# Feed-forward residual path earlier, softmax sums of the first block inverted once per value, six places for weight sums

## What is computed

```python
x = x + layernorm(attention(layernorm(x)))   # 16 heads of 16, weights alpha * sign(W), bias
x = x + layernorm(ffn(x))

def ffn(x):                                  # ternary weights, one scale per output
    h = silu(lin(x, w1)) * lin(x, w2)        # 256 -> 1024
    h = gelu(lin(h, h1))                     # 1024 -> 1024
    h = gelu(lin(h, h2))                     # 1024 -> 1024
    return lin(h, w3)                        # 1024 -> 256
```

## Time and profile before

| | us |
|---|---|
| median of three runs | 1197.16 |
| profiled execution, own time | 1199.53 |
| its span, first to last instruction | 1197.8 |
| PE busy | 1145.4 (96%) |
| ACT busy | 918.6 (77%) |
| DVE busy | 755.8 (63%) |
| last exponential of attention ends | about 549 |
| a middle feed-forward block | 80.2 |

### The profile page before, as it was taken

One profiled execution on the slowest core, in us unless ns is written; L12 is line 12 of the kernel. 1 busy time (PEld: TensorE's weight loads), 2 busy tenths in 40 slices (PEclk: granted clock), 3 DMA queues, 4 the chain that ended last, 5 costly groups with the idle time before them and its releaser, 6 DMA issues.

```text
span 1197.8 us, 21087 instructions
## 1 busy us (share of the span) xinstructions
PE 1145.4 (96%) x8241; PEld 778.0 (65%) x8241; DVE 755.8 (63%) x1165; ACT 918.6 (77%) x1218; POOL 88.6 (7%) x140
## 2 busy tenths in 40 slices
PE   6699999999999999898999999999999999999997
PEld 4233323332333322225999999989989999899897
DVE  7354525353436246895767767768678677686766
ACT  6689999999999999795675676757756766577565
POOL 6001000101010000000010000010100000101000
PEclk9799999999999999899999999999999999999999
DMA  5989768976899589834330431423404314233031
GB/s 180 238 213 230 190 103 194 225 182 103 198 212 202 103 187 199 221 123 152 100 138 30 142 125 61 151 92 110 141 35 141 125 55 145 101 110 138 4 124 55
DMA packets 67031, 166.96 MB, mean 139 GB/s; under 512 B 10102, under 2 KB 27126, under 8 KB 60774
## 3 DMA queue, kind: packets, MB, share of 16 engines
q1 hardware_dynamic: 66636, 165.12, 51.2%
q10 hardware_dynamic: 288, 0.39, 0.1%
HBM read 122.18 MB, written 52.40 MB: 146 GB/s over the span
## 4 chain that ended last, share of the span: by engine, by line
PE 32%; DVE 10%; ACT 6%; issue 3%; POOL 2%; DVEq 0%; ACTq 0%
PE ffn_ps L1876 21%; DVE op_lo L2130 4%; PE ffn_ps L1814 4%; PE ffn_ps L1815 4%; ACT op_hi L1991 3%; PE ffn_ps L1889 3%; ACT feed L2020 2%; PE side_ps L1781 1%; DVE feed L2123 1%; ACT zn L2026 1%; DVE ln_stats L2108 1%; DVE feed L2148 1%; ACT L2020 1%; POOL ln_shift L1701 1%; DVE feed L2141 1%
## 5 line engine op out<-in xcount | busy, mean ns | idle before, releaser
L1286 ACT ACTIVATE probs<-s_ps 128x1024 f32<-128x1024 f32 x512 | 475.5, 1115 | 36.0 <-PE s_ps L1131 35.4
L1145 PE MATMUL y_ps<-probs,v_st 128*17 128x512 f32 x2048 | 272.7, 605 | 9.1 <-DVE y_sb L1311 8.1
L1876 PE MATMUL ffn_ps<-op_hi,W 128*128 128x256 f32 x1024 | 240.5, 279 | 0.0
L1876 PE MATMUL ffn_ps<-op_lo,W 128*128 128x256 f32 x1024 | 240.5, 279 | 0.0
L2130 DVE TENSOR_TENSOR op_lo<-feed,op_hi 128x1024 fp32r<-128x1024 f32 x144 | 174.7, 1222 | 95.3 <-ACT op_hi L1991 95.3
L1131 PEld LDWEIGHTS s_ps<-q_st,k_st 50*128 50x128 f32 x1024 | 88.4, 187 | 209.9 <-ACT probs L1286 172.0
L1131 PE MATMUL s_ps<-q_st,k_st 50*128 50x512 f32 x1024 | 207.4, 470 | 7.8 <-DVE y_ps L1521 7.3
L1876 PEld LDWEIGHTS ffn_ps<-op_hi,W 128*128 128x128 f32 x1024 | 193.3, 189 | 0.3
L1876 PEld LDWEIGHTS ffn_ps<-op_lo,W 128*128 128x128 f32 x1024 | 191.7, 187 | 0.3
L1876 PE MATMUL ffn_ps<-op_hi,sums_of_w 128*128 128x256 f32 x768 | 186.8, 284 | 0.5 <-ACT feed L2007 0.5
L1876 PE MATMUL ffn_ps<-op_lo,sums_of_w 128*128 128x256 f32 x768 | 186.0, 283 | 0.0
(11 more groups left out here) (199 smaller groups left out, 1308.8 us busy)
## 6 DMA issues: line engine op xcount, KB each, us to landing
sums_of_w<-sum_scr SPq DMA_DIRECT2D x48, 1024.0 KB, 5.0
k_st<-qk_scr SPq DMA_DIRECT2D x90, 128.0 KB, 6.5
q_st<-qk_scr SPq DMA_DIRECT2D x90, 128.0 KB, 7.0
w_scr<-ffn_w SPq DMA_DIRECT2D x16, 704.0 KB, 8.0
W<-w_scr SPq DMA_DIRECT2D x16, 704.0 KB, 5.9
y_scr<-y_sb SPq DMA_DIRECT2D x32, 256.0 KB, 4.0
qk_scr<-y SPq DMA_DIRECT2D x24, 256.0 KB, 6.8
qk_scr<-sums SPq DMA_DIRECT2D x24, 256.0 KB, 7.9
```

The source lines that it names most:

```text
L1145: i = pe.matmul(y_ps[32 * j:32 * j + VCOLS, :], v_st[g % 2][:, s, VCOLS * j:VCOLS * (j + 1)], probs[(PAIRS * turn + j // 2) % PROBS][:, j ...
L1286: act.activation(probs[a % PROBS][:, :, :], s_ps[a % 3][:, :, :], ACT.Exp, scale=SCALE)\
L1876: mm = pe.matmul(dst[:, a * HB:(a + 1) * HB], w, part[slot][:, kt // 2, cols].bitcast(form), start=(fresh and kt == 0 and a == 0 and part ...
```

## The change

It has three parts.

1. `sum_at` has six places for the first 16 sums: the two new ones lie in the tile `zn`. Three semaphores instead of two tell of stored sums; `wait_sum_stores` waits for the first so many pairs of them. At turn 36, before `zn` is written with the projection, DVE waits for the first six pairs.
2. For the first block the sums are loaded once per value, 128 x 64 (`load_few_sums`), DVE inverts them with one instruction at turn 22, and at turn 24 SP waits for that, stores them in `inv_scr`, waits for the store and loads them spread over the rows, as the later blocks do. The four spread inversions and their two loads at turn 11 go.
3. In the feed-forward blocks the steps of the residual path take earlier places: on PE `project_y` from behind U2 to behind Z of layer 0, and `turn_x1` from between the two output pairs to behind C21 of layer 1; on ACT `normalise(Z)` from behind high(13) to behind high(10), `normalise(X1)` from behind high(15) to behind high(13), and the high part of x1 from behind high(17) to between the two gelus of Q12; on DVE the low part of y to behind low(3), and with it low(3) to before both halves of `add_c11`; scaling, bias, statistics, adding x and the low part of x1 as the diff shows. SP's order in these blocks is the same; its code moves into shared functions.

```diff
@@ -154,34 +154,38 @@
+def load_few_sums(sp, y_scr, few_sums, b, u, done):
+
+    y_blk = y_scr.rearrange("(b c a d) t -> b c a d t", b=BATCH, c=CT, d=2 * HEAD_DIM)
+    for c in range(CT):
+        few = y_blk[b, c, :, HEAD_DIM, u * BLK:(u + 1) * BLK].rearrange("a (s f) -> a s f", s=HEAD_DIM // 2)
+        sp.dma_start(few_sums[c * HALF:(c + 1) * HALF, :], few).then_inc(done, 16)
+
+
 def load_tail_y(sp, y_scr, tail_in, b, u):
     y_blk = y_scr.rearrange("(b c a d) t -> b c a d t", b=BATCH, c=CT, d=2 * HEAD_DIM)
-    tokens = slice(u * BLK, (u + 1) * BLK)
     for c in range(CT):
-        sp.dma_start(tail_in.y[:, c, :], y_blk[b, c, :, 0:HEAD_DIM, tokens]).then_inc(tail_in.y_loaded, 16)
-
-        sp.dma_start(tail_in.sums[:, c, :], y_blk[b, c, :, HEAD_DIM:HEAD_DIM + 1, tokens]
-                     .to_broadcast([P // HEAD_DIM, HEAD_DIM, BLK])).then_inc(tail_in.y_loaded, 16)
+        sp.dma_start(tail_in.y[:, c, :], y_blk[b, c, :, 0:HEAD_DIM, u * BLK:(u + 1) * BLK]).then_inc(tail_in.y_loaded, 16)
+
+
+def store_inverses(sp, inv_scr, few_sums, done):
+    sp.dma_start(inv_scr.rearrange("h (s f) -> (h s) f", s=HEAD_DIM // 2), few_sums).then_inc(done, 16)
+
+
+def spread_inverses(sp, inv_scr, tail_in):
+    for c in range(CT):
+        heads = HEADS // CT
+        sp.dma_start(tail_in.sums[:, c, :], inv_scr[c * heads:(c + 1) * heads, :].unsqueeze(1)
+                     .to_broadcast([heads, HEAD_DIM, BLK])).then_inc(tail_in.y_loaded, 16)
 TAIL_LOADS = 2 * CT
-
-
-INVERT_PARTS = 4
-
-
-def invert_sums(dve, tail_in, t, part):
-
-    if part == 0:
-        dve.wait_ge(tail_in.y_loaded, 16 * TAIL_LOADS * (t + 1))
-    n = CT * BLK // INVERT_PARTS
-    sums = tail_in.sums[:, :, :].rearrange("p c t -> p (c t)")[:, part * n:(part + 1) * n]
-    dve.reciprocal(sums, sums).then_inc(tail_in.inverted, 1)
+FEW = HEADS * BLK // P
 def divide_y(dve, tail_in, t):
-    dve.wait_ge(tail_in.inverted, INVERT_PARTS * (t + 1))
+    dve.wait_ge(tail_in.y_loaded, 16 * TAIL_LOADS * (t + 1))
     dve.tensor_tensor(tail_in.y[:, :, :], tail_in.y[:, :, :], tail_in.sums[:, :, :], ALU.mult)\
         .then_inc(tail_in.y_done, 1)
...
@@ -793,6 +797,7 @@
         qk = [sb(f"pj_qk{u}", [P, BLK], F32) for u in range(2)]
         group_top = sb("pj_group_top", [P, GROUPS], F32)
+        few_sums = group_top[:, 0:FEW]
         square = sb("pj_square", [P, QK, GROUPS], BF16)
         v_aug = sb("pj_v_aug", [P, HEADS // QUAD, TILES, QUAD, VCOLS], F32)
@@ -856,7 +861,9 @@
         sum_made = sem("sum_made")
         sum_checked = sem("sum_checked")
-        sum_stored = [sem(f"sum_stored{i}") for i in range(2)]
+        sum_stored = [sem(f"sum_stored{i}") for i in range(3)]
+        few_loaded = sem("at_few_loaded")
+        inv_stored = sem("at_inv_stored")
         Y_HI, Y_LO, Z_SCALED, Z_BIASED, Z_ADDED = 1, 2, 3, 5, 6
         block = ctx.enter_context(nc.Block())
@@ -874,9 +881,19 @@
         def sum_at(j):
-            if j % 4 < 2:
-                return qk[j % 4][:, :]
-            return v_aug[:, :, :, :, :].rearrange("p q t j n -> p (q t j n)")[:, (j % 4 - 2) * HM:(j % 4 - 1) * HM]
+            n = j % 6 if j < SUM_UNITS // 2 else j % 4
+            if n < 2:
+                return qk[n][:, :]
+            if n < 4:
+                return v_aug[:, :, :, :, :].rearrange("p q t j n -> p (q t j n)")[:, (n - 2) * HM:(n - 1) * HM]
+            return xb[:, :, :].rearrange("p t c -> p (t c)")[:, (n - 4) * HM:(n - 3) * HM]
+
+        def wait_sum_stores(eng, pairs):
+
+            for r in range(3):
+                n = len(range(r, pairs, 3))
+                if n:
+                    eng.wait_ge(sum_stored[r], 32 * n)
         def quarter_of_w(l, kt, m, k):
...
@@ -1008,7 +1025,13 @@
                     for i in range(2):
                         sp.wait_ge(part_stored[i], 16 * 2 * (QK // 2) * PROJECTED)
+                    load_few_sums(sp, y_scr, few_sums, 0, 0, few_loaded)
                     load_tail_y(sp, y_scr, tail_in, 0, 0)
+                if t == 24:
+                    sp.wait_ge(tail_in.inverted, 1)
+                    store_inverses(sp, inv_scr, few_sums, inv_stored)
+                    sp.wait_ge(inv_stored, 16)
+                    spread_inverses(sp, inv_scr, tail_in)
                 if t == 26:
                     sp.dma_start(tail_in.x1[:, :, :], x_blk[0]).then_inc(tail_in.x_loaded[0], 16)
...
@@ -1444,8 +1466,7 @@
                 a11, a12, a21, a22 = (quarter_of_w(l, kt, m, k) for m, k in ((0, 0), (0, 1), (1, 0), (1, 1)))
                 dst, prior = sum_at(j), sum_at(j - 1)
-                if j >= 4:
-                    dve.wait_ge(sum_stored[j // 2 % 2], 32 * (j // 4))
+                wait_sum_stores(dve, j // 2 - (2 if j < SUM_UNITS // 2 else 1))
                 if j:
                     dve.wait_ge(sum_made, j)
@@ -1471,8 +1492,9 @@
                 if t in SUM_TURNS:
                     sum_of_weights(SUM_TURNS.index(t))
-                if t in (24, 26, 28, 30):
-                    invert_sums(dve, tail_in, 0, (t - 24) // 2)
+                if t == 22:
+                    dve.wait_ge(few_loaded, 16 * CT)
+                    dve.reciprocal(few_sums, few_sums).then_inc(tail_in.inverted, 1)
                 if t == 32:
                     divide_y(dve, tail_in, 0)
@@ -1482,6 +1504,8 @@
                     dve.tensor_tensor(y_lo[:, :, :], tail_in.y[:, :, :], y_hi[:, :, :].bitcast(F32),
                                       ALU.subtract).then_inc(x1_steps, 1)
+                if t == 36:
+                    wait_sum_stores(dve, 6)
                 if t in (36, 38):
                     i, per_bank = (t - 36) // 2, TILES // CT
...
@@ -1927,13 +1942,14 @@
                 for k in range(NP):
                     product(i, 0, k)
-                    if ahead and k == K_U2:
+                    if ahead and k == K_Z:
                         project_y(i)
                 for k in range(NP):
                     product(i, 1, k)
+                    if ahead and k == K_C21:
+                        turn_x1(i)
                 if ahead:
                     out_tiles(i, 0)
-                    turn_x1(i)
                     out_tiles(i, 1)
                 else:
@@ -2070,6 +2086,8 @@
                 copy_c11(i, 1, 1)
                 high(i, 10)
+                if ahead:
+                    normalise(Z, i + 1, zn, zn, z_norm)
                 gelu(i, 1, Q11, 0)
                 gelu(i, 1, Q11, 1)
@@ -2080,21 +2098,19 @@
                 high(i, 13)
                 if ahead:
-                    normalise(Z, i + 1, zn, zn, z_norm)
+                    normalise(X1, i + 1, zn, x1[1 - u], x1_norm)
                 gelu(i, 1, Q22, 0)
                 gelu(i, 1, Q22, 1)
                 gelu(i, 1, Q21, 1)
                 high(i, 15)
+                gelu(i, 1, Q12, 0)
                 if ahead:
-                    normalise(X1, i + 1, zn, x1[1 - u], x1_norm)
-                gelu(i, 1, Q12, 0)
+                    high_of_x1(i)
                 gelu(i, 1, Q12, 1)
                 high(i, 16)
                 high(i, 17)
-                if ahead:
-                    high_of_x1(i)
             blocks(step)
@@ -2175,10 +2191,6 @@
                 dve.wait_ge(few_loaded, 16 * CT * (i + 1))
                 dve.reciprocal(few_sums[:, :], few_sums[:, :]).then_inc(few_inverted, 1)
-
-            def divide(i):
-                dve.wait_ge(tail_in.y_loaded, 16 * TAIL_LOADS * (i + 2))
-                dve.tensor_tensor(y[:, :, :], y[:, :, :], tail_in.sums[:, :, :], ALU.mult).then_inc(y_done, 1)
             def low_of_y(i):
@@ -2270,15 +2282,17 @@
                 make_t(i, 0, 2)
                 if ahead:
-                    divide(i)
+                    divide_y(dve, tail_in, i + 1)
                 make_t(i, 0, 3)
+                low(i, 3)
+                if ahead:
+                    low_of_y(i)
                 add_c11(i, 0, 0)
-                low(i, 3)
                 add_c11(i, 0, 1)
                 make_t(i, 0, 4)
                 low(i, 4)
                 if ahead:
-                    low_of_y(i)
+                    scale_z(i)
                 low(i, 5)
                 if behind:
@@ -2286,17 +2300,16 @@
                 add_c22(i, 0, 1)
                 if ahead:
-                    scale_z(i)
+                    bias_z(i)
                 low(i, 7)
                 if ahead:
-                    bias_z(i)
                     dve.wait_ge(z_done, i + 1)
                     stats_of(Z, zn, range(TILES))
                 add_c12(i, 0, 0)
                 low(i, 8)
-                add_c12(i, 0, 1)
                 if ahead:
                     mean_var_of(Z, i + 1)
+                add_c12(i, 0, 1)
                 make_t(i, 1, 1)
                 low(i, 9)
@@ -2306,24 +2319,25 @@
                 make_t(i, 1, 4)
                 low(i, 11)
+                if ahead:
+                    add_x(i, 1 - u, ahead[0])
                 low(i, 12)
+                if ahead:
```

(12 more changed lines are left out.)

31 lines of the change are left out of this document (11 added, 20 removed).

## The result

The changed kernel takes 1225.98 us (median of four runs, 1221.75 to 1229.84) against 1196.75 us (1195.18 to 1197.98) for the kernel before on the same chip: 1.0244 times as long, 95% interval 1.0207 to 1.0281. The forecast was 1214.7 with a range to 1224. The sign was right, the size was 11 us short, and the median lies 2 us outside the range. One run further down, of the kernel with one wait filled, took 1375.79 us at a mean granted clock of 0.75 and is in no median.

A forecast was written before the change was run, and what follows sets the result against it. The matrix engine was taken to bound the feed-forward part, ACT's exponentials the attention part. Terms -7.2 + 10.4 + 0.3 + 14.0 = +17.5 us on a median of 1197.2 gave 1214.7 us, range 1200 to 1224.

The forecast's parts named there:

- Attention: Attention part: gaps of 4.68 and 0.66 us close and 1.8 us of the other four goes; gain 7.2 us.
- Layer 0: Feed-forward blocks 1 to 6: add_c11 behind low of y delays U2's copy and U3; loss 1.73 us each, 10.4 us together.
- Layer 1: Feed-forward, seven blocks: second output pair released later, its gap growing from 1.5 to about 2.8 us; loss 2.0 us each, 14.0 together.
- The string: Layer 1: ACT's unbroken work from normalising x1 at 697.28, crossing DVE twice, puts the second output pair at 711.30.
- POOL's part: Layer 1: normalising x1 waits for POOL's rstd and shift, 2.89 us after mean and variance end.
- the rule: POOL contends with two-input SBUF instructions on VectorE: first POOL item would wait for low(13), sum the same within 0.1 us.
- rival D: Widened gap before the second output pair lowers the clock: 1.7 us per block, 1226 us if in each; chance 0.12.
- My gap of 2.8 us: Forecast idle time of PE before layer 1's second output pair, about 2.8 us where it was 1.5.
- the likeliest case: The forecast itself, whole kernel: +17.5 us, 1214.7 us; chance 0.60.
- A: Layer 1 goes as meant, -0.9 us per block, while layer 0 costs 10.7: 1194.4 us; chance 0.13.
- B: Nothing is lost in layer 0 and layer 1 is won: 1183 us; chance 0.07.
- C: Layer 0 is free, layer 1 costs 14 us: 1204 us; chance 0.08.

## Why the prediction failed, point by point

- Attention: -7.2 forecast, -7.3 in the profiled pair, -5.0 by the ratio of medians. That the pair agrees to 0.1 us is in part luck, since another trace with the attention part of before ends it 2.65 us sooner. The gaps of 4.68 and 0.66 us closed, and of the other four 1.5 of 3.5 us went (0.47, 0.93 and 0.67 are left), where I took 1.8. The copy of turn 33 was forecast near 481 and came at 481.22; the division, forecast with the spreads at 477 to 479, started at 478.20. Where I was wrong without consequence: I had both edits work together, and either does it alone.
- Layer 0: 1.73 us per block forecast, 1.76 measured. The copy of U2 started at 660.44, that is 665.97 with 5.53 us added (forecast 665.99), and U3 likewise at 666.70 (forecast 666.72). The projection before them idled 0.10 us and not 0.3. The cause is shown by the kernel with add_c11 first. Block 0 has no such wait, as forecast, and in block 7 it grew from 0.52 to 0.80.
- Layer 1: 2.0 us per block forecast, 1.78 measured (83.74 - 80.20 - 1.76), of which 0.63 + 2.40 - 1.48 = 1.55 stand in the listed waits. ACT started normalising x1 after 3.9 us idle, forecast some 4. With 5.53 us added and layer 0's 1.73 taken off it began at 697.10 (forecast 697.28), and the second pair at 711.11 (forecast 711.30). The string was right to 0.2 us: from the end of mean and variance (690.59) POOL's items took 2.71 us to the normalising, where the forecast had taken over 2.89. These 0.2 us, seven times, are most of the 1.4 us by which the waits were forecast too long (24.7 against 23.3). That high and low of x1 are the larger part of it is shown by the kernel that moves them back.
- POOL's part: the trace agrees with what the Trainium skill says of the shared interface (GPSIMD Engine Reference, Specifications). The first small item after the mean and variance now took the long time and ended with the subtraction of low(13) on DVE (690.50 to 691.69), and the last took 0.20 where it had taken 1.26. The forecast had this as what the rule would bring:

```profile
690.67 1.09 POOL L1720 TENSOR_TENSOR ln_std<-ln_mean_var,ln_eps_row 128x4 f32<-128x4 f32 x1 [14.73 <-DVE ln_mean_var L2130]
...
693.07 0.20 POOL L1725 TENSOR_TENSOR ln_shift<-ln_neg_mean,ln_rstd 128x4 f32<-128x4 f32 x1
```

- The step that failed is the one between forecast and rival D: the sum has no term for the clock. "My gap of 2.8 us is of that size", and yet the likeliest case kept the clock at its upper level and D had 0.12. The forecast's own gap was as long as one that had just brought the clock down in the trace of before, and the only row against it was a shorter one of 1.48 us. In its place the runs show six falls of 1.55 us, 9.3 us in the profiled run, and 8.3 us by the ratios. With D's own price, 1.7 us a block, six falls and the sum of +17.5 give 1225 us; measured 1225.98. That this comes so near is luck in part: by the ratios the attention part gained 2.2 us less than forecast and the waits cost 1.3 more (26.0 against 24.7). The top of the range, "D in most blocks", was built on a probability that the rows did not support, and stood below D's own 1226.
- What could not be had from the trace of before is that the falls came in six blocks of seven here and in one of seven elsewhere, and that the very wait of 2.80 us on which D rested has a fall beside it in six traces of thirteen. A fair forecast was then D as likely as not. The Trainium skill (TensorE: Matmul & The Clock Gate, section on HAM oscillation) speaks of the transition being paid anew at each of repeated idle stretches, in a case with DMA waits of 3 to 5 us, longer than the waits here. The runs agree that it repeats, at 1.55 us each, and show beyond it that not every stretch of one length pays.

Rivals A, B and C are ruled out by the rows of block 1: the second pair waits longer and not less, and U3 waits.

## What to carry to other kernels

In an in-order queue a small step moved earlier delays all that stands behind it. Before moving it, look for the next instruction of that queue for which the bounding engine waits: two steps of 0.95 and 1.22 us cost 1.9% here. Where a forecast has waits of the bounding matrix engine at all of the length that brought its clock down somewhere in the trace, count the fall as one of two even cases (here six traces of thirteen for one such wait), with its price per occurrence, and let the range hold all of them. Two edits that both remove the lateness of one copy are worth one.

## What the runs showed of the hardware

- Waits of 1.74 to 1.76 us were followed by 3.4 us at the lower clock nine times (four in the kernel with one wait filled, one with the split of x1 last, four with longer blocks), while waits of 2.4 us left the clock untouched in six blocks of seven in another. Each fall cost 1.55 us of matmuls of 128x256.
- The same wait of 2.82 us, in kernels with the same program up to it, had a fall beside it in one trace (clock 0.50 from 543.70 on) and none in another (1.00).
- Filling both waits with matmuls whose results nobody reads kept the clock at 1.00 (0.69%, 8.3 us here) and left the block at 83.73 us. Filling one of them left four falls at the other.
- The small POOL items of 128x4 at L1720, L1721 and L1725 take 0.20 us by themselves. Where one starts beside a DVE instruction of 128x1024 with two inputs in SBUF it ends 0.06 us behind that one: it took 1.09 to 1.26 us where both started together, and 0.38 where the DVE instruction had 0.32 us left (before, 679.31). Beside an addition with an input in PSUM (L2183) L1721 took 0.20. The item that makes rstd (L1723) took 1.01 us each time.
